# Turning the row maxima one pair of scores later, and a swap in GpSimd's order, in a fused attention and expert kernel

## The reference, cut to what matters

```python
query, key = qt_c + rope(qt_r), kt_c + rope(kt_r)      # (16, 16 heads, 256, 8)
attn = softmax(einsum('bhqd,bhkd->bhqk', query, key) / scale)
x = x + einsum('bhqk,bhkd->bhqd', attn, value) @ Wo_w + Wo_b
...
topv, topi = top_k(layernorm(x) @ gate_w + gate_b, 2)  # of 24 experts
for e in range(24):
    h = gelu(xt @ w1[e] + b1[e], approximate=False)
    out = out + cw[:, e:e + 1] * (h @ w2[e] + b2[e])
```

## Time and profile before

| | |
|---|---|
| median of 3 runs | 706.02 us (704.02 to 712.03) |
| the profiled execution | 712.84 us, its span 711.0 us |
| mean granted TensorE clock in it | 0.835 of full speed |
| TensorE matmuls busy | 549.7 us, 77% of the span |
| VectorE busy | 418.6 us, 59% |
| GpSimd busy | 347.9 us, 49% |
| ScalarE busy | 345.2 us, 49% |

### The profile page before, as it was taken

One profiled execution on the slowest core, in us unless ns is written; L12 is line 12 of the kernel. 1 busy time (PEld: TensorE's weight loads), 2 busy tenths in 40 slices (PEclk: granted clock), 3 DMA queues, 4 the chain that ended last, 5 costly groups with the idle time before them and its releaser, 6 DMA issues. The chain is left out here.

```text
span 711.0 us, 16954 instructions
## 1 busy us (share of the span) xinstructions
PE 549.7 (77%) x4220; PEld 391.4 (55%) x4221; DVE 418.6 (59%) x1199; ACT 345.2 (49%) x879; POOL 347.9 (49%) x613
## 2 busy tenths in 40 slices
PE   4598697888897789789788887510799999999920
PEld 3444454554554455446355443210799999899920
DVE  6384666766785786677676674240455555455526
ACT  1224554654565565466465445200355555555533
POOL 6642635555555656555545542212255555455522
PEclk9657889898899998889898676555899999999965
DMA  6323333433434433332443522195222222122045
GB/s 203 93 87 102 103 111 118 121 94 116 136 93 125 135 104 108 119 119 96 124 143 95 171 81 71 35 342 204 66 70 61 62 61 62 55 65 60 17 153 202
DMA packets 63443, 77.86 MB, mean 110 GB/s; under 512 B 7794, under 2 KB 51067, under 8 KB 62768
## 3 DMA queue, kind: packets, MB, share of 16 engines
q1 hardware_dynamic: 56816, 66.47, 30.9%
q0 software_dynamic: 4864, 8.54, 3.6%
q10 hardware_dynamic: 1728, 2.43, 1.0%
HBM read 50.98 MB, written 27.61 MB: 111 GB/s over the span
## 5 line engine op out<-in xcount | busy, mean ns | idle before, releaser
L908 DVE TENSOR_REDUCE mx<-s 128x2 f32<-128x512 f32 x256 | 171.1, 685 | 109.1 <-PE s L534 84.9
L763 ACT ACTIVATE pr<-s 128x512 f32<-128x512 f32 x256 | 148.1, 598 | 143.8 <-PE s L553 122.9
L885 ACT ACTIVATE pr<-s,wts 128x128 f32<-128x128 f32 x352 | 100.3, 368 | 90.0 <-PE s L730 81.4
L1409 POOL DMA_INDIRECT results<-pr,ridx x88 | 98.6, 1120 | 87.7 <-issue 46.5
L534 PE MATMUL s<-w 72*128 72x256 bf16 x512 | 114.9, 312 | 5.0 <-DVE mx L908 2.2
L553 PE MATMUL s<-w 75*128 75x256 bf16 x512 | 112.4, 307 | 1.9 <-ACT pr L763 1.4
L565 PE MATMUL pv<-pr,vm 128*32 128x256 f32 x1024 | 96.5, 457 | 0.0
L738 PE MATMUL s<-w,pr 128*128 x704 | 93.3, 275 | 2.3 <-ACT pr L885 2.3
L1336 POOL DMA_INDIRECT dispatched<-pay,pos x64 | 63.1, 986 | 57.5 <-DMA dispatched<-qkp 20.6
L738 PEld LDWEIGHTS s<-w,pr 128*128 128x128 f32 x704 | 85.7, 192 | 2.9 <-issue 2.9
L534 PEld LDWEIGHTS s<-w 72*128 72x128 bf16 x512 | 46.2, 110 | 64.5 <-issue 29.8
(11 more groups left out here) (158 smaller groups left out, 822.1 us busy)
## 6 DMA issues: line engine op xcount, KB each, us to landing
w<-parts_out SPq DMA_DIRECT2D x32, 288.0 KB
w<-parts_out SPq DMA_DIRECT2D x96, 96.0 KB
w<-in_w SPq DMA_DIRECT2D x16, 512.0 KB, 4.2
parts_out<-qkp SPq DMA_DIRECT2D x16, 384.0 KB
tin<-dispatched SPq DMA_DIRECT2D x88, 66.0 KB
weighed_out<-weighed_sb SPq DMA_DIRECT2D x16, 256.0 KB, 2.1
w<-in_w SPq DMA_DIRECT2D x4, 1024.0 KB
w<-results SPq DMA_DIRECT2D x8, 512.0 KB, 7.4
```

The lines of the kernel that those rows point to most:

```text
L763: nc.scalar.activation(pr[h // NG % 2][:, h % NG, :, :], s2[h % 2][:, :, :], ACT.Exp, scale=SCALE).then_inc(exp_done, 1)
L885: last = nc.scalar.activation(hT[t.pair][:, c, :], hps[t.pair][:, :, :].rearrange("p a s -> p (a s)")[:, c * P:(c + 1) * P], ACT.Gelu, bia ...
L908: nc.vector.tensor_reduce(mx[j % 2][:, :, g], s1[h % 2][:, :, :], AX.X, ALU.max).then_inc(max_done, 1)
L1409: nc.gpsimd.indirect_dma_start(results, bass.IndirectOffsetOnAxis(ap=ridx[t.slot][:, 0:1], axis=0), yo[t.slot], None, bounds_check=TOPK * ...
```

## The change

The matmuls that turn a quarter's maxima are issued behind the pair of scores at g = 2 instead of g = 1, and ScalarE's copy of them stands ahead of the exponents of g = 3 instead of g = 2. On GpSimd, `third_part` moves from before the splits of the third quarter to behind them.

```diff
@@ TensorE, step
                     if held.attend:
                         pass2(b, s, h)
-                    if g == 1 and turns(held, q):
+                    if g == 2 and turns(held, q):
                         turn_max(*turning(b, s, q))
@@ ScalarE, step
                     q, g = divmod(h, NG)
-                    if g == 2 and turns(held, q):
+                    if g == 3 and turns(held, q):
                         m, _, j = turning(b, s, q)
                         take_maxima(m, j)
                     if held.attend:
@@ GpSimd, step
                 if held.project:
                     leave(b + 2)
-                    third_part(b + 2)
                 if held.lead:
                     split_maxima(*turning(b, s, 2)[::2])
+                if held.project:
+                    third_part(b + 2)
                 if held.send:
                     send(b - 2, s)
```

## The result

The changed kernel is slower: 714.26 us median (706.19 to 723.45, 20 runs) against 707.11 us (703.19 to 714.68, 20 runs). The ratio is 1.007 with a 95% interval of 1.0037 to 1.0102. The profiled execution has a span of 712.3 us and a mean granted clock of 0.815, where before had 711.0 and 0.835.

A forecast was written before the change was run, and what follows sets the result against it. No one engine bounds a round; the GpSimd chain limits the fourth quarter's turn. 24.80 - 1.5 - 0.15 + 1.5 (clock) = 24.65 us against 25.63, 10.8 us over 11 rounds, plus 1: 12 us off 706.0 gives 694.0 us, range 680 to 711.

The forecast's parts named there:

- The GpSimd chain: GpSimd's own work from the third quarter's split end to the fourth's, 7.67 us; TensorE's fourth-quarter turn cannot come before its end.
- the third quarter's wait of 1.77 us: TensorE's wait ahead of the third quarter's turn; it goes, but shortens no round.
- The fourth quarter's turn: Work moved ahead of this turn lets ScalarE start normalise_rows 1.5 us earlier, at 325.8 instead of 327.28.
- the whole round at full clock: A round of 24.80 us less 1.5 (fourth quarter's turn) and 0.15 (second quarter's turn) becomes 23.15 us.
- the two new waits: TensorE's fourth-quarter waits: for the split, 1.5 to 3.3 us, then for normalise_rows, 1.4 us.
- `third_part` behind the splits: On GpSimd, third quarter: the split goes first, send begins at 316.66 instead of 316.87, the chain starts 0.2 us earlier.
- The clock: Falls behind the fourth quarter's waits cost the next first quarter 1.5 us a round, with ends of 0 and 3.4.
- The row that I leaned on: A stretch to the next turn after a 1.46 us wait: 7.60 us at clock 0.78, against 6.40 at 1.00.
- a row with a fall of 6.7 us: A stretch from 316.7 to 323.4 us at clock 0.51, behind the third quarter's wait; priced 3.4 us if all exposed.
- The last rival: The clock falls for the next round's whole first quarter: 3.4 us cost, round 26.55 us, kernel 716 us; chance 0.12.
- The other rounds: Rounds 0, 1, 13 and 14 have fewer of these waits and other limits; 1 us gained together.
- The rival from the Trainium skill: The clock holds behind the fourth quarter since activity releases it: round 23.15 us, gain 28 us, 678 us; chance 0.12.

The follow-up runs named there:

- e5_before_fill: The kernel before with idle products: three ahead of the turns of the third and fourth quarter, one ahead of x2_turned; 699.87 us, ratio 0.979.
- e3_fill: The changed kernel with idle fp32 products in the fourth quarter's waits, three ahead of the turn, two ahead of x2_turned; 674.52 us, ratio 0.956.
- e2_turn: The kernel before with only the later turn and copy, third_part staying ahead of the splits; 714.43 us, ratio 1.011.
- e11_turn_fill: The kernel before with only the later turn and copy, plus five idle products in the fourth quarter's waits; 681.45 us, ratio 0.957.
- e9_thin: The changed kernel with five idle products in the same places and the same added waits, each only 16 by 16; 716.42 us, ratio 1.005.
- e10_tail: The changed kernel with the five idle products, and three, five and eight more ahead of project_out in rounds 13 to 15; 670.91 us, ratio 0.941.

## Why the prediction was wrong

It forecast 694 us and faster; measured were 714 and slower. By its own steps:

*The GpSimd chain, and that the third quarter's wait of 1.77 us is worth nothing:* right. The wait went, and in ten of eleven rounds the fourth quarter's stands in its place. In round 5 the chain still takes 8.7 us from one split's end to the next (177.05 to 185.71 us), as said.

*The fourth quarter's turn, 1.5 us, and the whole round at full clock, 23.15 us:* right in kind, too large in size. `normalise_rows` starts right behind its shift. But where the sum takes 1.65 us off a round, single rounds at full clock show 1.2 (24.80 in e5_before_fill, 23.60 in e3_fill) and the eleven rounds together 1.04; round 4 takes 23.50 us. The first of the two new waits was put at 1.5 to 3.3 us and the second at 1.4; they measure 1.5 and 1.2 us on average.

*`third_part` behind the splits, 0.2 us:* right with the early turn (24.8 to 24.6), nothing with the late one.

*The clock:* this is the step that failed. The text had the place right, the first quarter of the next round at full price, but took "1.5 us, near the one fall that a row prices". Measured against the same order with the clock held, it is 26.78 - 23.79 = 3.0 us a round (294.6 and 261.7 us for eleven rounds), twice that, near the 3.4 us that stood as the upper end. In the order before, the clock cost 25.63 - 24.83 = 0.8 us a round. So the whole is: 1.0 us gained by the order and 2.2 us more lost to the clock, which makes the 1.15 us by which a round is longer. Of the 2.1 us between the forecast's 24.65 and the measured 26.78, 1.5 are the clock's and 0.6 the order's.

The row that I leaned on (7.60 against 6.40 us) was of a single fall, part of which lay in TensorE's slack. I had also a row with a fall of 6.7 us and set it aside, because TensorE was busy in it and the clock then rose. But in round 7 TensorE is busy at half clock for all 9.90 us of the first quarter and the clock does not rise sooner, and in round 3 not for 25 us. The last rival was thus what happened in the rounds, "the clock falls for the whole first quarter": 26.78 us against its 26.55. A chance of 0.12 was far too small for it, and the range ended at 711 because a case with 0.12 was allowed to be cut. That its 716 us came so near the 714 measured is in part luck. It counted nothing outside rounds 2 to 12, and in the profiled pair all the rest is 11.4 us shorter than before, which leaves a difference of 1.3 us where the medians have 7.

*The other rounds, 1 us:* mis-sized. Rounds 0 and 1 took 54.6 us before and 50.6 in e5_before_fill, which puts no idle products there; the changed kernel took 40.2 and e3_fill 41.8. That looks like a gain of 10 us from the change, but it is not shown to be one. These are rounds 0 and 1 of e2_turn and of e11_turn_fill, which have the same instructions in them:

```profile
44.40:84.80 40.40, 36.03 (x302) 21.40 (x302) 30.42 (x70) 26.65 (x57) 21.16 (x51) 0.98 0.47 142
44.40:93.40 49.00, 46.20 (x301) 25.53 (x301) 30.82 (x71) 26.94 (x57) 21.07 (x51) 0.74 0.39 118
```

They differ by the clock, from execution to execution. Rounds 13 to 15 lost 6.4 us in the profiled pair, at a clock of 0.64 against 0.72, which is one execution of each and not settled.

*The rival from the Trainium skill,* page "TensorE: Matmul & The Clock Gate", Part 1, by which activity releases the clock: e3_fill against e9_thin agrees, 0.99 against 0.78, where the work in the waits is the only difference. But it did not help the changed kernel that TensorE waits less ahead of turns (14.9 us instead of 39.8): its clock in rounds 2 to 12 is 0.82, and was 0.89.

## What to carry to other kernels

A wait that leaves one place turns up where the chain behind it ends; ask not only whether it is shorter there but what the clock does behind it, and whether the next stretch has slack. Before, the falls lay largely under GpSimd's own work and cost 0.8 us a round; gathered ahead of the one quarter that TensorE bounds, they cost more than the better order brought. When a reordering ought to help and does not, put idle work of real size into TensorE's waits first: it separates the order's worth (here 1.0 to 1.4 us a round) from the clock's (3.0). Here it was itself worth 2% on the kernel before (e5_before_fill), and together with the new order 4 to 6% (e3_fill, e10_tail).

## What was not expected of the hardware

TensorE's clock stayed at half through 9.90 us in which TensorE was busy for 9.90 us, and in two traces through 25 us of which it was busy in all: in round 4 of e2_turn, shown above, and in round 3 of the changed kernel.

```profile
109.50:134.50 25.00, 25.00 (x129) 14.01 (x127) 14.62 (x36) 10.89 (x24) 10.26 (x18) 0.50 0.32 95
```

Other stretches at half clock ended sooner, after 6.7 us in the earlier trace rows. Busy time in the profile therefore doesn't tell when the clock comes back. What in these rounds keeps it down was not tried.
